# An adaLN block on one core: the second normalization applied behind its transpose by ScalarE, its statistics by matmul, bias ranks moved to steps 30 to 33, two of three causal masks added by TensorE

## What is computed

```python
mod = (_silu(L0_c) @ L0_wmod).reshape(L0_c.shape[0], 6, 1, -1)
sa, ca, ga, sb, cb, gb = (mod[:, 0], mod[:, 1], mod[:, 2], mod[:, 3], mod[:, 4], mod[:, 5])
...
h = _layernorm(x, axis=-1) * (1 + ca) + sa
x = x + ga * _L0_attn_ref(h, L0_attn_W_qkv, L0_attn_W_o)
h = _layernorm(x, axis=-1) * (1 + cb) + sb
x = x + gb * _L0_ffn_ref(h, ...)
# in _L0_attn_ref: scores - slopes * rel, causal mask, softmax
# in _L0_ffn_ref:
h = (x - mu) * jax.lax.rsqrt(var + 1e-05) * ln_gamma + ln_beta
logits = jnp.einsum('bsh,he->bse', h, Wr) + br
tier = jnp.where(a >= thr_top, -1.0, jnp.where(a <= thr_bot, 1.0, 0.0))
return w + scale * w * tier
```

## Time and profile before

| | |
|---|---|
| median of three runs | 238.66 us (238.48 to 248.0) |
| the profiled execution | 239.84 us, its span 238.1 us |
| granted TensorE clock, mean | 0.978 |
| start to the first PV | 0 to 42.8 us |
| PV of steps 6 to 37 | 42.8 to 178.4 us |
| f2(0) to the end of the span | 184.9 to 238.1 us |
| DMA traffic | 20.9 MB, 88 GB/s |

### The profile page before, as it was taken

One profiled execution on the slowest core, in us unless ns is written; L12 is line 12 of the kernel. 1 busy time (PEld: TensorE's weight loads), 2 busy tenths in 40 slices (PEclk: granted clock), 3 DMA queues, 4 the chain that ended last, 5 costly groups with the idle time before them and its releaser, 6 DMA issues.

```text
span 238.1 us, 5477 instructions
## 1 busy us (share of the span) xinstructions
PE 216.5 (91%) x1901; PEld 152.5 (64%) x1918; DVE 185.0 (78%) x562; ACT 162.6 (68%) x344; POOL 143.6 (60%) x223
## 2 busy tenths in 40 slices
PE   8977989899899899889879879979879999999993
PEld 3554757676676676666667556735535878766793
DVE  4767899889799899998998876974967585675464
ACT  2577658989989989979669769937628741453320
POOL 8650232758979979988666236437779608283600
PEclk9997999999999999999999999999985999999999
DMA  6668665965948137237036000000000001010011
GB/s 179 118 185 224 153 168 140 243 183 143 249 120 211 41 95 213 53 96 194 6 89 181 26 0 6 0 0 6 3 0 3 0 3 44 0 45 3 0 44 44
DMA packets 19461, 20.90 MB, mean 88 GB/s; under 512 B 1547, under 2 KB 17562, under 8 KB 18370
## 3 DMA queue, kind: packets, MB, share of 16 engines
q1 hardware_dynamic: 18746, 20.22, 32.5%
q10 hardware_dynamic: 688, 0.33, 0.5%
HBM read 15.16 MB, written 5.26 MB: 86 GB/s over the span
## 4 chain that ended last, share of the span: by engine, by line
PE 63%; DVE 18%; ACT 7%; issue 7%; POOL 4%; ACTq 0%; DVEq 0%; POOLq 0%
PE bank L918 12%; PE bank L898 10%; PE bank L819 6%; DVE nmax L1208 4%; PE bank L715 4%; PE bank L776 4%; ACT msk L599 3%; PE bank L798 3%; PE bank L881 3%; PE bank L772 3%; PE bank L952 3%; PE bank L824 2%; DVE msk L1183 2%; PE bank L932 2%; PE bank L930 2%
## 5 line engine op out<-in xcount | busy, mean ns | idle before, releaser
L494 POOL TENSOR_SCALAR_AFFINE_SELECT PT<-PT 128x256 f32<-128x256 f32 (+1 forms) x96 | 46.8, 502 | 35.0 <-ACT PT L584 32.8
L599 ACT ACTIVATE msk<-wa,cand 128x1024 bf16<-128x1024 f32 (+1 forms) x62 | 57.7, 941 | 5.3 <-DVE cand L1194 5.3
L584 ACT ACTIVATE PT<-bank 128x512 f32<-128x512 f32 x96 | 55.5, 607 | 5.0 <-PE bank L793 3.4
L1208 DVE TENSOR_REDUCE nmax<-bank 128x2 f32<-128x512 f32 x64 | 43.5, 685 | 2.5 <-PE bank L776 1.8
L460 POOL TENSOR_TENSOR ex<-eul,lg 128x32 f32<-128x32 f32 x4 | 21.7, 5436 | 17.2 <-DVE lg L1270 17.2
L1204 DVE TENSOR_REDUCE nmax<-bank 128x4 f32<-128x512 f32 x32 | 21.7, 677 | 4.3 <-PE bank L769 4.2
L776 PE MATMUL bank<-Ks,Qs 78*128 78x256 bf16 x128 | 24.8, 276 | 0.0
L798 PE MATMUL bank<-Qs,Ks 80*128 80x256 bf16 x128 | 24.5, 273 | 0.2 <-ACT PT L584 0.2
L1183 DVE TENSOR_SCALAR_CACHE_REDUCE msk<-wa,cand 128x512 bf16<-128x512 f32 x31 | 23.1, 746 | 1.1
L819 PE MATMUL bank<-PT,Vx 128*32 128x256 f32 x256 | 20.9, 398 | 1.6 <-POOL PT L494 1.0
L772 PE MATMUL bank<-mask 128*128 128x256 bf16 x64 | 18.0, 281 | 2.9 <-DVE nmax L1208 2.4
(11 more groups left out here) (196 smaller groups left out, 489.6 us busy)
## 6 DMA issues: line engine op xcount, KB each, us to landing
Qs<-parts SPq DMA_DIRECT2D x7, 576.0 KB
Ks<-parts SPq DMA_DIRECT2D x7, 576.0 KB
parts<-part SPq DMA_DIRECT2D x7, 384.0 KB, 2.8
rows_bc<-rows_out SPq DMA_DIRECT2D x8, 192.0 KB, 7.9
x_all<-in_x SPq DMA_DIRECT2D x8, 128.0 KB, 7.0
parts<-part SPq DMA_DIRECT2D x8, 128.0 KB, 2.9
out<-ob SPq DMA_DIRECT2D x3, 256.0 KB, 2.3
wa<-in_w SPq DMA_DIRECT2D x2, 256.0 KB, 4.6
```

The lines of the kernel that those rows point to most:

```text
L494: gp.affine_select(out=v, in_=v, compare_op=ALU.is_ge, fill=0.0, base=0, pattern=[[0, v.shape[1]], [1, P]], channel_multiplier=-1).then_in ...
L584: act.activation(PT[:, e % 2, j], psE[u % 2][:, :], ACT.Exp).then_inc(q["exp_done"], 1)
L599: act.activation(scratch, wa[:, 0:width], ACT.Sign, bias=cand[:, col:col + 1].bitcast(F32), scale=-(1.0 - 2.0 ** -24), accum_out=acc[:, co ...
L1208: ve.tensor_reduce(nmax[:, b % 2, 1, h:h + 2], bank.rearrange("p (h k) -> p h k", h=2), axis=AX.X, op=ALU.max, negate=True).then_inc(q["ma ...
```

## The change

**Masks.** Of the three exponentials of a group, the two with 256 queries (j = 1, 2) get their causal mask before the exponential: PE adds -1e30 above the diagonal to the scores by one bf16 matmul of 2x128 columns with the mask as weights. POOL's select stays for j = 0.

**n2.** second_use and router_stats go. PE turns n2, and ACT's copy to h2T applies scale (1 + cb) and offset sb, which are now columns (mod2T), once per batch. The router's mean becomes a ninth column of wrg (1/128), its mean square comes from the squares of h2T (DVE, `squares`) by four one-column matmuls (fp32), and `router_moments` makes mean, variance and the centred logits from them. The variance's power stands on POOL ahead of each exponential. Only the ga and gb rows are broadcast by DMA, gb late.

**Biases.** b1 is compared on DVE (four masks with a count in the accumulator) at step 31, its ranks are 16 matmuls at step 32, and it is perturbed at step 33; b2's masks move to step 30.

**Order.** The x_all add stands ahead of the division into A. w_o is loaded by SP, and turned after the first projection. c_pe_l(0) moves from step 36 to step 33.

The diff's core, by engine:

```diff
@@ gpsimd, the loop @@
-                    for j in range(3):
-
-                        gp.wait_ge(q["exp_done"], 3 * e + j + 1)
...
+                    gp.wait_ge(q["exp_done"], 3 * e + 1)
+                    v = PT[:, e % 2, 0].rearrange("p (h q) -> p h q", h=HG)
+                    gp.affine_select(out=v, in_=v, compare_op=ALU.is_ge, fill=0.0, base=0,
+                                     pattern=[[0, HG], [1, P]], channel_multiplier=-1).then_inc(q["sel_done"], 1)
...
-                if t in B1_AT:
-                    bias_masks(B1_AT.index(t))
@@ scalar, c_act_h @@
+                    act.wait_ge(q["sq_done"], p - 1)
+                for k in range(2):
+                    b = 2 * p + k
+                    act.activation(h2T[:, p % 2, S * k:S * (k + 1)], (psE[1] if p >= 2 else psQ)[:, S * k:S * (k + 1)], ACT.Identity,
+                                   scale=mod2T[:, 1, b:b + 1], bias=mod2T[:, 0, b:b + 1]).then_inc(q["h2T_done"], 1)
@@ tensor, e_unit and pv @@
+                    mm(bank.rearrange("p (h k) -> p h k", h=2)[:, :, 0:P], mask5[:, 0, :],
+                       mask5[:, HG, :].unsqueeze(1).broadcast_to([P, 2, P]), start=True, stop=False, skip_group_check=True)
                     for i in range(2):
                         h = HG * g + 2 * (j - 1) + i
                         last = mm(bank[:, i * S:(i + 1) * S], Ks[0:R_E, r, h, 0:P], Qs[0:R_E, r, h, :],
-                                  start=True, stop=True, skip_group_check=True)
+                                  start=False, stop=True, skip_group_check=True)
...
-                pe.wait_ge(q["sel_done"], 3 * e + 3)
+                pe.wait_ge(q["sel_done"], e + 1)
+                pe.wait_ge(q["exp_done"], 3 * e + 3)
@@ tensor, c_pe_l @@
+                pe.wait_ge(q["sq_done"], p + 1)
+                for i in range(4):
+                    last = mm(psX[:, MSQ_COLS + i:MSQ_COLS + i + 1], sq[:, i * P:(i + 1) * P], wrg[:, NE:NE + 1], start=True, stop=True)
+                last.then_inc(q["sq_sum"], 1)
@@ tensor, the loop @@
+                if t == BIAS_STEP + 1:
+
+                    pe.wait_ge(q["b1m_done"], 1)
+                    claim_x((q["b1p_done"], 1))
+                    for m in range(NC):
                         for j in range(NC):
...
+                if t == MOMENT_STEP - 1:
                     c_pe_l(0)
@@ vector @@
+            def squares(p):
+
+                v.wait_ge(q["h2T_done"], 2 * (p + 1))
+                if p:
+                    v.wait_ge(q["sq_sum"], p)
+                ve.tensor_tensor(sq[:, :], h2T[:, p % 2], h2T[:, p % 2], op=ALU.mult).then_inc(q["sq_done"], 1)
...
+            def bias_masks():
+
+                v.wait_ge(q["b1abs_done"], 1)
+                for i in range(NC):
+                    last = ve.tensor_scalar(rmask[:, i], b1a[:, :], colsa[:, i:i + 1], 0.0, op0=ALU.is_gt, op1=ALU.add,
+                                            accum_out=b1_over[:, i:i + 1])
+                last.then_inc(q["b1m_done"], 1)
...
             for n in range(2 * NPAIR):
                 combine(n)
                 p = n // 2 + 1
-                if p < NPAIR:
-                    (router_weights if n % 2 else router_logits)(p)
+                if p < NPAIR and n % 2 == 0:
+                    squares(p)
+                    router_moments(p)
+                    router_logits(p)
+                elif p < NPAIR:
+                    router_weights(p)
```

More of the change, by code:

```diff
@@ L974, in _ @@
             mm(psE[1][0:B, 0:512], c_s[:, :], wmod_sb[:, 2 * D:6 * D], start=True, stop=True).then_inc(q["pe_set"], 1)
+            pe.wait_ge(q["dve_set"], SETS["modT"])
+            for j in range(2):
+                last = mm(psE[0][:, j * B:(j + 1) * B], wmod_sb[:, (3 + j) * D:(4 + j) * D], c_s[:, :], start=True, stop=True)
+            last.then_inc(q["pe_set"], 1)
             turned(1)
@@ L1004, in _ @@
                     total(n)
+                if first and t in AHEAD and t >= B * G:
+                    f1_ahead(*AHEAD[t])
                 pv(t)
@@ L1011, in _ @@
                 e_unit(t, 2)
-                if t in AHEAD and t >= B * G:
+                if t in AHEAD and t >= B * G and not first:
                     f1_ahead(*AHEAD[t])
+                if t in F1_STEPS:
+                    f1(1, F1_STEPS[t])
                 ut(t)
@@ L1410, in _ @@
                     router_logits(0)
+                b = batch_at(t, AT_Y)
+                if b is not None:
+                    v.wait_ge(q["y_done"], b + 1)
+                    ve.tensor_tensor(x_all[:, b], x_all[:, b], psX[:, 0:S].rearrange("p (i d) -> p i d", i=NBLK),
+                                     op=ALU.add).then_inc(q["x2_done"], 1)
                 b, g, e = lagged(t, E_LAG + 1)
@@ L1455, in _ @@
                     perturb_b2()
-            second_use(B - 1)
-            router_stats(B - 1)
+                if t == SQUARE_STEP:
+                    squares(0)
+                if t == MOMENT_STEP:
+                    router_moments(0)
             router_weights(0)
```

237 lines of the change are left out of this document (96 added, 141 removed).

## The result

The changed kernel takes 251.85 us (median of four runs, 251.22 to 252.71); beside it the kernel before took 239.13. The ratio is 1.0544, with a 95% interval from 1.0489 to 1.0599: slower by 5.4%. The profiled execution took 251.45 us, with a span of 249.7.

What follows compares the result with a forecast made beforehand. The prediction took TensorE alone to bound the tail and no single engine the loop. Its terms, -2.4 + 1.1 + 7.9 + 2.0 = +8.6 us, gave 247.3 us on the median, range 242.5 to 252.5.

Steps and rivals of the forecast that it cites:

- its two terms: Tail, from f2(0) to the end: +7.9 us for transposed statistics and waits, +2.0 for one fall of the clock.
- The three waits for sq: Tail, pairs 1 to 3: TensorE waits for DVE's squares some 1.6, 2.8 and 1.2 us.
- The matmuls on the squares: Tail, each pair: four one-column fp32 matmuls, priced at 0.79 us like the four of eight columns.
- the term of 7.9: Tail: waits and statistics matmuls add 2.3, 3.6 and 2.0 us at pairs 1, 2 and 3; bounds 6.5 to 9.
- The clock: Tail: one fall of TensorE's clock among the three waits, +2.0 us (0 to +5).
- Steps 31 to 39: Ahead of f2(0): waits for b2p and lg_read, less 1.5 us taken back, delay f2(0) by +1.1 us (0 to +3.5).
- The loop: Loop: masks +3.0, PV's waits -1.0, DVE contention -1.2, moved bias work -3.2; -2.4 us (-6 to +4).
- Start of f2(0): Start of the tail: -2.4 us from the loop and +1.1 from steps 31 to 39.
- The clock stays: Rival, tail: clock stays at 1.00 through the waits; +6.6 us, 245.3 us; chance 0.20.
- Relief wins in the loop: Rival: POOL and DVE held the loop, which gains 5.5 us; tail costs 7, total +1.5, 240.2 us; chance 0.16.
- PE becomes the bound and the clock falls at each wait: Rival: masks +6, steps 31 to 39 +3, tail 8, clock 5, less 5.4; +16 us; chance 0.10.

Runs made afterwards that it cites:

- e2: Changed kernel with spare 384-column matmuls filling TensorE's waits for the squares of pairs 1, 2 and 3: 247.02 us, ratio 1.0277.
- e8: Changed kernel with all exponential masks back on GpSimd, b2's chain early and the three squares early: 238.24 us, ratio 0.9901.
- e7: Changed kernel with b2's chain alone moved ahead, sizes and masks to step 24, rank matmul to 26, perturbation to 27: 250.15 us, ratio 1.0503.
- e6: Changed kernel with reciprocal and A again ahead of the x_all add on DVE: 251.26 us, ratio 1.0567.
- e9: Kernel before with the bias work moved, but DVE's b1 masks spread over steps 22, 24, 26, 29, sizes and b2 masks in 7 and 23: 234.57 us.
- e11: Kernel before with only b1's rank matmuls and perturbation moved to steps 32 and 33, its masks left on GpSimd: 236.86 us, ratio 0.9859.
- e5: Kernel before with the whole bias work alone moved as in the changed kernel; exponential masks, statistics and tail as before: 235.84 us, ratio 0.9875.
- e4: Changed kernel with the mask change alone taken back, GpSimd selecting all three exponential units again: 251.71 us, ratio 1.0473.
- e3: Kernel before with the mask change alone: TensorE masks exponential units 1 and 2, GpSimd selects unit 0 only: 238.48 us, ratio 0.9964.

## Why the prediction was right, and where it was off

I predicted 247.3 us, 242.5 to 252.5, and slower by more than 2% with 0.77. It is slower, and 251.85 lies in the range, near its upper end. The likeliest number was 4.6 us too low. Between the two profiled executions the difference is 11.6 us where the sum had 8.6. The tail took 4.0 more than its two terms (13.9 for 9.9) and the stretch ahead of it 2.0 more, while the loop gave 2.7 more and the start 0.4. So the number owes part of its place in the range to errors that offset each other, which is luck. Point by point:

- **The three waits for sq.** Predicted about 1.6, 2.8 and 1.2 us; measured 1.82, 2.61 and 1.22. The order combine, squares, matmuls, and at pair 2 combine(1), router_weights(1), combine(2) ahead of the squares, stands in the trace as it was worked out.
- **The matmuls on the squares.** Priced at 0.8 us a group by the router matmuls. They take 1.05 right behind a wait (pair 3 of the changed kernel) and 1.04 behind the spare matmuls of e2, and 0.89 behind the router's (e8). Three of them are 3.2 and not 2.4. With the waits that makes 8.8 for the term of 7.9; e2's tail is 8.9 longer than before.
- **The clock: the term that was mis-sized.** I wrote that a fall costs 1.7 or 3.5 us and took one among the three waits. The sizes were right: 1.7 at pair 1 (1.45 in f1, 0.23 in the matmuls ahead of it) and 3.4 at pair 2. The count was wrong, both happened. Which pair pays which is not fixed: in e7, with the same waits, pair 1 lost 3.1 us (1.87 for 1.05 in the matmuls on the squares, 5.81 for 3.54 in f1) and pair 2 1.7. The tail lost 5.0 by the clock, shown by e2, where 2.0 stood in the sum.
- **Steps 31 to 39.** The waits for b2p (predicted 2.9, measured 2.08) and for lg_read (2 against 0.71) came where they were said to. That a fall of the clock could follow the first was not in the sum. It did, from 159 to 165.6 us, and cost some 3 us; e7 takes wait and fall away and gains 4.6 us between PV 32 and f2(0), and e6, with the wait and no fall, has 2.9 of them. The 1.5 us that the sum took back here were mostly for the fall of the kernel before at 177 us, which did go; e9 and e11, without it, are 2.0 us shorter in this stretch. The stretch lost 3.1 us where 1.1 was predicted.
- **The loop.** Predicted -2.4, measured -5.1, inside the bounds. Along the chain of kernels before, e11, e5, e4, changed, the stretch goes 118.1, 114.6, 111.6, 110.8, 113.0. The rank waits gave 3.5 (predicted 3.2). GpSimd out of DVE's way gave 1.4; the sum had 1.2, though half of 0.7 us for each of four batches, as its working has it, is 1.4. The masks cost 2.2 net (predicted 3.0 less the 1.0 for PV). What has no term in the prediction is the rest. 1.6 lie between e11 and e5 behind PV 22, half of it around the b2 masks that left step 23. 0.8 lie between e5 and e4, which differ above all in two things: h2 and its statistics leave DVE, and the add stands ahead of A. e6 measured the second at 0.7, so most of this may be the order; it is not shown which. I had priced all of these at nothing.
- **Start of f2(0).** The last two errors offset each other: f2(0) starts 2.3 us earlier (182.41 for 184.75), and -2.4 + 1.1 said 1.3.
- **The rivals.** "The clock stays" is out for the tail: of the three waits only pair 3's, the shortest, left it alone. "Relief wins in the loop" had the loop's 5.5 us nearly right, and it did not help, since the tail took more. What happened lies closest to the last rival, "PE becomes the bound and the clock falls at each wait": TensorE is busy 16.91 of 17.34 us of a batch, and the clock fell behind its three longest waits. I gave it 0.10. That its 252 is the time measured says nothing for it: it had +6 for the masks, and its sum does not give 252. All of +16 would be 254.7 on the median, and half of it 246.7, not "252 and more".

The rule that I weighed against the trace, that the fall belongs to a stretch of idleness (the Trainium skill, TensorE: Matmul & The Clock Gate, Part 1), would have given 245.3 as I read it, with waits broken by small matmuls costing nothing. That reading was too narrow, for the same part also tells of a kernel in which brief idleness between groups of matmuls made the clock go down and up. The measurement decides against my reading here: at pairs 1 and 2 the router matmuls stood ahead of the wait and the ones on the squares behind it, and f1 took 4.99 and 6.50 us.

The other rule, on a VectorE instruction with two SBUF inputs beside a GpSimd one that reads SBUF (the Trainium skill, SBUF — State Buffer, Who interferes with whom), agrees in kind: the subtraction into nmHL has a median of 304 ns before and 192 in e3, where GpSimd selects a third as many units. The cast, which has one input, shortens as well, 352 to 182; the same section names casts among the instructions that can contend with GpSimd, in their two-port modes. Whether this one ran in such a mode no run here shows.

## What to carry to other kernels

Ask of every wait that an edit puts on the engine at the end of the chain what that engine does right behind it, and price the wait twice: once for its length, once for the clock of the work that follows. Here the second price was nearly as large as the first (5.0 against 5.6 us in the tail). If such a wait cannot be avoided, filling it with spare matmuls is worth trying, since it gave the 5.0 us back without making anything ready sooner.

An edit that bundles several moves is worth taking apart even if it is slower: of this one, the bias work alone made the kernel 1.3% faster (2.1% with its masks spread, which is not told apart from the first), while statistics that had been off TensorE's path were moved onto it.
